# Attention stage of a macaron transformer layer: the softmax normalization is emitted one query tile later

## The chip, the cores and the metric

The kernel runs on all 8 cores of one Trainium2 chip. Each core takes one of the 8 sequences (2048 tokens x 1024 features) and computes the whole layer for it; the cores exchange nothing. The metric is device microseconds of the slowest core; lower is better.

## What is computed

```python
x = x + 0.5 * ffn(layernorm(x), W_fc, W_proj)
x = x + attn(layernorm(x), gamma, Wq, Wkv, Wo)
x = x + 0.5 * ffn(layernorm(x), W_fc, W_proj)

# ffn: h = relu(x @ W_fc.T)**2 ; y = h @ W_proj.T ; then a 5-step spiking
#      threshold on y (here five comparisons with constants)
# attn: 16 heads of 64, one shared key/value head, causal:
sim = einsum('bhid,bjd->bhij', q * SCALE, k)
sim = where(j > i, -max, sim)
out = einsum('bhij,bjd->bhid', softmax(sim), v)
return out.reshape(B, S, 1024) @ Wo
```

## The kernel before

The program is written as five instruction streams, one per engine: T (TensorE, PE), V (VectorE, DVE), A (ScalarE, ACT), S (SyncE, which issues DMAs) and G (GpSimd). `P.emit` appends an instruction to a stream and may raise a semaphore; `P.wait` makes a stream wait for a semaphore's value. Each engine executes its stream in the order in which it was emitted, so the order of the Python code is the order of the work.

Three stages follow each other: a feed-forward block, attention, and the second feed-forward block. The change is in the attention stage alone.

The attention loop goes over 16 query tiles (`qt`, 128 queries each). Tile `qt` needs keys 0 to `(qt+1)*128`, which are cut into `jbn` units of up to 512 keys: 1 unit for tiles 0 to 3, 2 for 4 to 7, 3 for 8 to 11, 4 for 12 to 15, 40 units in all. Only the last unit of a tile holds the diagonal; its width N is 128, 256, 384 or 512 columns.

For one unit:
- T computes the scores of 8 head pairs (lines 725, 730) into two alternating pairs of PSUM banks (0 to 3); a pair waits for the exponentials of the pair before the last, and for `v_mc` (line 723), which is raised inside the latest normalization.
- In the diagonal unit V adds a triangular mask (line 738) before A may read.
- A computes the exponential (line 753) into a buffer of WB and adds up the row sums in `sacc`. The first exponential of a tile waits for V's memset of its half of `sacc` (line 710, semaphore `v_sz`). `sacc` has two halves, by the parity of `qt`.
- S issues one DMA transpose for the whole unit (line 767) once all its exponentials are done and the previous unit's `emit_av` has freed the destination, which all units share.
- T multiplies the transposed exponentials with the values (`emit_av`, line 650), 4 matmuls per 128 keys, into banks 4 and 5 for even tiles and 6 and 7 for odd ones. This is emitted one unit late: after the scores of unit u comes `emit_av` of unit u-1.

When a tile's last unit has been through `emit_av`, `emit_msc(qt)` normalizes the tile: V reduces and inverts the row sums (lines 662, 666), T transposes them with 8 small matmuls (672), V copies (677, 680), T spreads them over the partitions with two matmuls (684), V copies again (689) and raises `v_mc` (692), and V multiplies the two output banks into HB (697, semaphore `v_msc`). It borrows the score banks that were used last, so T waits for all exponentials emitted so far (line 670). `emit_av` of a tile's first unit waits for `v_msc` of the tile before the last, whose banks it reuses.

After the loop come the output projection (line 798) and the second feed-forward block.

Of the kernel before, what the change touches and what calls it, by code (L numbers as in the profile page):

```python
# [61 lines left out]
def build_program(S=2048, stage="full"):  # L62
# [77 lines left out]
    def qs_t(pc, t0, n=512, p0=0, pn=128):  # L140
        return Q3[p0:p0 + pn, pc * S + t0: pc * S + t0 + n]
# [16 lines left out]
    def kt2_t(t0, n=512, p0=0, pn=128):  # L158
        return WB[p0:p0 + pn, KTP + t0: KTP + t0 + n]
# [4 lines left out]
    def p2_t(par, pc, hl, n=512):  # L164
        base = (P0P if par == 0 else P1P) + (pc * 2 + hl) * n
        return WB[:, base: base + n]
# [10 lines left out]
    def msc_t(c0, n):  # L177
        return WB[:, MSP + c0: MSP + c0 + n]

    def r2_t(c0, n):  # L180
        return WB[0:2, R2P + c0: R2P + c0 + n]
# [272 lines left out]
    def attention():  # L454
# [169 lines left out]
        unit_of = {}  # L624
        uidx = 0
        pend_av = None
        pend_msc = None

        def emit_av(qt, jb, u):
            ext = (qt + 1) * 128  # L630
# [26 lines left out]
        def emit_msc(qt):  # L657
            ob = 4 if qt % 2 == 0 else 6
            spb = 2 * (1 - (P.val("t_s") // 2) % 2)
            P.wait("V", "a_ex", ex_done[qt])  # L660
            po = (qt % 2) * 64
            P.emit("V", lambda E, po=po: E.tensor_reduce(
                rs16[:], sacc[:, po:po + 64].rearrange("p (g j) -> p g j", j=4),
                axis=mybir.AxisListType.X, op=ALU.add))
            P.drain("V")
            P.emit("V", lambda E: E.reciprocal(rs16[:], rs16[:]),
                   inc=("v_rs", 1))
            P.drain("V")
            P.wait("T", "v_rs", qt + 1)
            P.wait("T", "a_ex")  # L670
            for pc in range(NP):
                P.emit("T", lambda E, pc=pc, mb=spb: E.transpose(  # L672
                    PB[mb + pc // 4][0:2, (pc % 4) * 128:(pc % 4) * 128 + 128],
                    rs16[:, pc * 2: pc * 2 + 2], ident),
                    inc=("t_mst", 1) if pc == NP - 1 else None)
            P.wait("V", "t_mst", qt + 1)
            P.emit("V", lambda E, mb=spb: E.tensor_copy(  # L677
                r2_t(0, 512), PB[mb][0:2, 0:512]))
            P.drain("V")
            P.emit("V", lambda E, mb=spb: E.tensor_copy(  # L680
                r2_t(512, 512), PB[mb + 1][0:2, 0:512]), inc=("v_r2", 1))
            P.wait("T", "v_r2", qt + 1)
            for half in range(2):
                P.emit("T", lambda E, half=half, mb=spb: E.matmul(
                    PB[mb + half][:, 0:512], e2[:], r2_t(half * 512, 512),
                    start=True, stop=True), inc=("t_msm", 1) if half else None)
            P.wait("V", "t_msm", qt + 1)
            for half in range(2):
                P.emit("V", lambda E, half=half, mb=spb: E.tensor_copy(
                    msc_t(half * 512, 512), PB[mb + half][:, 0:512]))  # L690
                P.drain("V")
            P.emit("V", lambda E: E.engine_nop(), inc=("v_mc", 1))
            P.wait("V", "t_av", unit_of[(qt, ((qt + 1) * 128 + 511) // 512 - 1)] + 1)
            for half in range(2):
                dstbase = half * 4 * S + qt * 128
                dst3 = bass.AP(HB, dstbase, [[HB.shape[1], 128], [S, 4], [1, 128]])
                P.emit("V", lambda E, half=half, ob=ob, dst3=dst3: E.tensor_tensor(
                    dst3,
                    PB[ob + half][:, 0:512].rearrange("p (pc n) -> p pc n", n=128),
                    msc_t(half * 512, 512).rearrange("p (pc n) -> p pc n", n=128),  # L700
                    op=ALU.mult), inc=("v_msc", 1))
                P.drain("V")

        for qt in range(NQT):
            ext = (qt + 1) * 128
            jbn = (ext + 511) // 512
            par = qt % 2
            po = par * 64
            P.wait("V", "a_ex")
            P.emit("V", lambda E, po=po: E.memset(sacc[:, po:po + 64], 0.0),  # L710
                   inc=("v_sz", 1))
            for jb in range(jbn):
                u = uidx
                uidx += 1
                unit_of[(qt, jb)] = u
                upar = u % 2
                N = min(512, ext - jb * 512)
                for pc in range(NP):
                    i = P.val("t_s") // 2
                    bA = (i % 2) * 2  # L720
                    bB = bA + 1
                    P.wait("T", "a_ex", max(0, P.val("a_ex") - 2))
                    P.wait("T", "v_mc")
                    P.emit("T", lambda E, pc=pc, qt=qt, jb=jb, N=N, bA=bA:
                           E.matmul(PB[bA][:, 0:N],  # L725
                                    qs_t(pc, qt * 128, 128, 0, 64),
                                    kt2_t(jb * 512, N, 0, 64),
                                    start=True, stop=True))
                    P.emit("T", lambda E, pc=pc, qt=qt, jb=jb, N=N, bB=bB:
                           E.matmul(PB[bB][:, 0:N],  # L730
                                    qs_t(pc, qt * 128, 128, 64, 64),
                                    kt2_t(jb * 512, N, 64, 64),
                                    start=True, stop=True), inc=("t_s", 2))
                    diag = qt * 128 - jb * 512
                    if 0 <= diag < N:
                        P.wait("V", "t_s")
                        for b in (bA, bB):
                            P.emit("V", lambda E, b=b, diag=diag: E.tensor_add(  # L738
                                PB[b][:, diag:diag + 128],
                                PB[b][:, diag:diag + 128], tri[:]),  # L740
                                inc=("v_msk", 1))
                            P.drain("V")
                    if 0 <= diag < N:
                        P.wait("A", "v_msk")
                    P.wait("A", "t_s")
                    if jb == 0 and pc == 0:
                        P.wait("A", "v_sz")
                    if u >= 2 and pc == 0:
                        P.wait("A", "s_tr", tr_done[u - 2])
                    for hl in range(2):  # L750
                        g = pc * 2 + hl
                        P.emit("A", lambda E, hl=hl, par=upar, jb=jb, N=N,
                               b=(bA, bB)[hl], pc=pc, g=g, po=po: E.activation(  # L753
                                   p2_t(par, pc, hl, N), PB[b][:, 0:N],
                                   AF.Exp, bias=ncb[:, pc:pc + 1], scale=1.0,
                                   accum_out=sacc[:, po + g * 4 + jb:
                                                  po + g * 4 + jb + 1]),
                               inc=("a_ex", 1))
                P.wait("S", "a_ex")
                P.wait("S", "t_av", u)  # L760
                jcn = N // 128
                srcbase = P0P if upar == 0 else P1P
                src2 = bass.AP(WB, srcbase, [[WB.shape[1], 128], [1, 16 * N]])
                dst3 = bass.AP(WB, 0,
                               [[WB.shape[1], 128], [128, 16 * jcn], [1, 128]])
                P.emit("S", lambda E, dst3=dst3, src2=src2:
                       E.dma_start_transpose(dst3, src2), inc=("s_tr", 16))
                tr_done[u] = P.val("s_tr")
                if pend_av is not None:
                    pqt, pjb, pu = pend_av  # L770
                    emit_av(pqt, pjb, pu)
                    pext = (pqt + 1) * 128
                    if pjb == (pext + 511) // 512 - 1:
                        emit_msc(pqt)
                pend_av = (qt, jb, u)
            ex_done[qt] = P.val("a_ex")
        pqt, pjb, pu = pend_av
        emit_av(pqt, pjb, pu)
        emit_msc(pqt)
# [149 lines left out]
```

How the kernel before makes its waits and increments, by code:

```python
        def run(E, SEM, fn=fn, inc=inc):  # L45
            ins = fn(E)
            if inc is not None:
                ins.then_inc(SEM[inc[0]], inc[1])
# [2 lines left out]
    def wait(self, eng, name, val=None):  # L51
        v = self.val(name) if val is None else val
        if v <= 0:
            return
        self.streams[eng].append(
            lambda E, SEM, name=name, v=v: E.wait_ge(SEM[name], v))
```

## Time and profile before

| | us |
|---|---|
| median of 2 timed runs | 2202.68 (2197.27 to 2208.09) |
| profiled execution | 2202.2 |
| its span, slowest core (core 1) | 2200.7 |
| spans of the 8 cores | 2173.4 to 2200.7 |
| the attention loop on core 1 | about 907 to 1581 |

Busy shares of the span: PE 66%, PE weight loads 26%, DVE 36%, ACT 28%, POOL 4%. In the attention loop PE's granted clock reads 0.5 to 0.6 of full speed in most slices, while the feed-forward stages read 0.7 to 1.0. All numbers of the timeline are microseconds from the span's start on core 1. In a timeline row, the bracket holds the time for which the engine sat idle before the instruction, and what released it.

### The profile page before, as it was taken

Reading aid. Unit: us, or ns where it says so; the run is one execution under the profiler, and the core shown is the slowest. Engines: PE = TensorE matmul, PEld = TensorE weight load, DVE = VectorE, ACT = ScalarE, POOL = GpSimd, SP = SyncE. Lnnn points to the kernel's source line nnn. Section 1 sums busy time; section 2 is a strip of 40 time slices with the busy share of each in tenths; the row PEclk is TensorE's granted clock in tenths of the full one; section 3 lists DMA queues with packets and bytes.
Section 4 is the critical chain, followed back from the end, with each engine's and each line's share of the span. In section 5 each row is a group of like instructions: output and inputs, shape, how many; then the busy total and the mean of one; then the engine's idle time right before and its main releaser. Section 6 shows DMA issues by size and latency. Waiting matters only on the chain.

```text
span 2200.7 us, 20979 instructions; the slowest of 8 cores (2173.4 to 2200.7 us)
## 1 busy us (share of the span) xinstructions
PE 1448.8 (66%) x6244; PEld 574.2 (26%) x6244; DVE 790.6 (36%) x1530; ACT 616.2 (28%) x1644; POOL 78.2 (4%) x151
## 2 busy tenths in 40 slices
PE   0396769999963465344544554455494999999992
PEld 0032224444420111111111111111141444444441
DVE  0430056372536444443222111111145226363526
ACT  0320011111203000345565665667203303020200
POOL 2000100000020000000000000000100000000000
PEclk9788879999987879755555555565697999999996
DMA  9808912213050111054555666656722031313231
GB/s 234 159 1 210 194 36 64 99 39 115 36 123 3 22 22 21 10 86 86 111 106 109 118 121 124 115 110 130 157 75 89 7 134 49 134 65 121 78 110 58
DMA packets 315791, 202.54 MB, mean 92 GB/s; under 512 B 288394, under 2 KB 288522, under 8 KB 304418
## 3 DMA queue, kind: packets, MB, share of 16 engines
q1 hardware_dynamic: 293586, 104.28, 22.8%
q0 software_dynamic: 20944, 88.52, 15.1%
q10 hardware_dynamic: 1152, 8.39, 1.3%
q8 instruction: 55, 0.90, 0.2%
q14 instruction: 54, 0.44, 0.1%
HBM read 125.76 MB, written 25.25 MB: 69 GB/s over the span
## 4 chain that ended last, share of the span: by engine, by line
PE 49%; DMA 18%; DVE 16%; ACT 10%; issue 6%; DVEq 1%; POOL 0%; SPq 0%; ACTq 0%; POOLq 0%
PE pb L439 18%; PE pb L385 14%; ACT WB L753 8%; DMA WB<-WB 7%; PE pb L650 5%; DVE acc L332 4%; PE pb L533 3%; PE pb L798 3%; DMA Q<-wprojT 2%; DMA X<-xin 2%; DMA Q<-wp 2%; PE pb L725 1%; DMA R_t<-r_d 1%; ACT Q L391 1%; DVEq L59 1%
## 5 line engine op out<-in xcount | busy, mean ns | idle before, releaser
L385 PE MATMUL pb<-Q,WB 128*128 128x512 bf16 x2048 | 457.0, 384 | 84.0 <-DVE Q L360 55.8
L439 PE MATMUL pb<-HB,Q 128*128 128x512 bf16 x2048 | 452.7, 383 | 50.4 <-DMA Q<-wprojT 32.0
L753 ACT ACTIVATE WB<-pb,ncb 128x512 bf16<-128x512 f32 (+3 forms) x640 | 389.6, 643 | 243.4 <-PE pb L730 126.9
L391 ACT ACTIVATE Q<-pb 128x512 bf16<-128x512 f32 x256 | 152.9, 597 | 756.8 <-PE pb L385 672.0
L725 PE MATMUL pb<-WB,Q 64*128 64x512 bf16 (+3 forms) x320 | 153.1, 501 | 274.9 <-ACT WB L753 247.8
L385 PEld LDWEIGHTS pb<-Q,WB 128*128 128x128 bf16 x2048 | 199.3, 98 | 340.6 <-issue 112.5
L439 PEld LDWEIGHTS pb<-HB,Q 128*128 128x128 bf16 x2048 | 200.1, 99 | 303.0 <-issue 73.7
L394 DVE TENSOR_TENSOR HB<-Q 128x512 bf16<-128x512 bf16 x256 | 105.1, 424 | 191.6 <-ACT Q L391 184.5
L738 DVE TENSOR_TENSOR pb<-pb,tri 128x128 f32<-128x128 f32 x256 | 76.7, 300 | 251.5 <-PE pb L730 235.5
L730 PE MATMUL pb<-WB,Q 64*128 64x512 bf16 (+3 forms) x320 | 159.0, 520 | 0.0
L650 PE MATMUL pb<-WB 128*64 128x512 bf16 x544 | 122.5, 624 | 46.1 <-DMA WB<-WB 45.9
L753 ACT ACTIVATION_READ_ACCUMULATOR WB<-pb,ncb 128x1 f32 x640 | 143.4, 224 | 0.0
L332 DVE SCALAR_TENSOR_TENSOR acc<-pb,acc 128x512 f32<-128x512 f32 x192 | 132.9, 692 | 14.3
L725 PEld LDWEIGHTS pb<-WB,Q 64*128 64x128 bf16 x320 | 30.2, 101 | 407.3 <-issue 405.6
L227 PE MATMUL pb<-Q,ones 128*1 128x512 bf16 x96 | 40.3, 419 | 116.2 <-DVE Q L219 115.9
L224 ACT ACTIVATE Q<-X 128x512 bf16<-128x512 f32 x96 | 56.4, 623 | 208.8 <-PE pb L231 159.5
L445 DVE COPY ysb<-pb 128x512 f32<-128x512 f32 x8 | 5.5, 692 | 258.2 <-PE pb L439 258.1
L357 DVE TENSOR_TENSOR acc<-X,MU_t 128x512 f32<-128x512 f32 x64 | 44.3, 692 | 142.3 <-DMA R_t<-r_d 136.7
L677 DVE CAST WB<-pb 2x512 bf16<-2x512 f32 x16 | 10.9, 678 | 225.0 <-PE pb L672 225.0
L650 PEld LDWEIGHTS pb<-WB 128*64 128x64 bf16 x544 | 45.9, 165 | 105.8 <-issue 105.8
L219 DVE CAST Q<-X 128x512 bf16<-128x512 f32 x96 | 39.7, 423 | 74.0 <-DMA X<-xin 50.6
L798 PE MATMUL pb<-HB,WB 128*128 128x512 bf16 x256 | 57.5, 389 | 10.1 <-DMA WB<-wo 10.1
(89 smaller groups left out, 777.6 us busy)
## 6 DMA issues: line engine op xcount, KB each, us to landing
Q<-wp POOLq DMA_DIRECT2D x56, 1024.0 KB, 6.1
X<-xin SPq DMA_DIRECT2D x8, 1024.0 KB, 27.3
WB<-wfcT POOLq DMA_DIRECT2D x16, 512.0 KB, 50.8
Q<-wprojT POOLq DMA_DIRECT2D x32, 256.0 KB, 13.4
wp<-Q SPq DMA_DIRECT2D x8, 1024.0 KB, 9.0
wf<-WB ACTq DMA_DIRECT2D x8, 1024.0 KB, 15.9
WB<-wf POOLq DMA_DIRECT2D x8, 1024.0 KB, 20.2
xout<-X SPq DMA_DIRECT2D x32, 256.0 KB, 2.2
```

The lines of the kernel that those rows point to most:

```text
L332: P.emit("V", lambda E, dc=dc, i=i: E.scalar_tensor_tensor(acc[:], ysrc(), THETA[i], acc[:], ALU.is_ge, ALU.add))
L385: P.emit("T", lambda E, par=par, dc=dc, fc=fc: E.matmul(PB[par][:], wfc_t(dc, fc), xn_t(dc)[:], start=(dc == 0), stop=(dc == DC - 1)), inc ...
L391: P.emit("A", lambda E, par=par: E.activation(hh_t(par)[:], PB[par][:], AF.Relu), inc=("a_rl", 1))
L394: P.emit("V", lambda E, par=par, fc=fc: E.tensor_mul(h_t(fc), hh_t(par)[:], hh_t(par)[:]), inc=("v_h", 1))
L439: st=st, sp=sp: E.matmul(PB[dc][:], wpe_t(par, fcl, dc), h_t(fc), start=st, stop=sp), inc=mark)
L533: P.emit("T", lambda E, oc=oc, dc=dc, bank=bank: E.matmul(PB[bank][:], wq_t(dc, oc), a_t(dc)[:], start=(dc == 0), stop=(dc == DC - 1)), in ...
L650: st=st, sp=sp, ob=ob: E.matmul(PB[ob + half][hl * 64:(hl + 1) * 64, 0:512], vb_t(jc), rhs, start=st, stop=sp, skip_group_check=True, tile ...
L725: E.matmul(PB[bA][:, 0:N], qs_t(pc, qt * 128, 128, 0, 64), kt2_t(jb * 512, N, 0, 64), start=True, stop=True))
L730: E.matmul(PB[bB][:, 0:N], qs_t(pc, qt * 128, 128, 64, 64), kt2_t(jb * 512, N, 64, 64), start=True, stop=True), inc=("t_s", 2))
L738: P.emit("V", lambda E, b=b, diag=diag: E.tensor_add(PB[b][:, diag:diag + 128], PB[b][:, diag:diag + 128], tri[:]), inc=("v_msk", 1))
L753: b=(bA, bB)[hl], pc=pc, g=g, po=po: E.activation(p2_t(par, pc, hl, N), PB[b][:, 0:N], AF.Exp, bias=ncb[:, pc:pc + 1], scale=1.0, accum_ou ...
L798: P.emit("T", lambda E, pc=pc, dc=dc, tt=tt, bank=bank: E.matmul(PB[bank][:], wo_t(pc, dc), outT_t(pc, tt * 512, 512), start=(pc == 0), st ...
```

## The change

The pending normalization becomes a list. Where `emit_msc` was called right after a tile's last `emit_av`, the tile is now appended to the list. The list is emptied at the top of each tile, ahead of its memset, and once more after the loop, ahead of the last `emit_av`. Inside a tile, ahead of each `emit_av`, it is emptied down to one entry. `emit_msc` itself and everything else stay.

```diff
-        pend_msc = None
+        pend_msc = []
...
             po = par * 64
+            while pend_msc:
+                emit_msc(pend_msc.pop(0))
             P.wait("V", "a_ex")
             P.emit("V", lambda E, po=po: E.memset(sacc[:, po:po + 64], 0.0),
                    inc=("v_sz", 1))
...
                 tr_done[u] = P.val("s_tr")
+                while len(pend_msc) > 1:
+                    emit_msc(pend_msc.pop(0))
                 if pend_av is not None:
                     pqt, pjb, pu = pend_av
                     emit_av(pqt, pjb, pu)
                     pext = (pqt + 1) * 128
                     if pjb == (pext + 511) // 512 - 1:
-                        emit_msc(pqt)
+                        pend_msc.append(pqt)
                 pend_av = (qt, jb, u)
             ex_done[qt] = P.val("a_ex")
+        while pend_msc:
+            emit_msc(pend_msc.pop(0))
         pqt, pjb, pu = pend_av
         emit_av(pqt, pjb, pu)
         emit_msc(pqt)
```

## Rows read from the trace of the kernel before

**Rows 1.** The page: chain that ended last, by engine, whole span
```profile
PE 49%; DMA 18%; DVE 16%; ACT 10%; issue 6%; DVEq 1%; POOL 0%; SPq 0%; ACTq 0%; POOLq 0%
```
**Rows 2.** The chain cut to 905 to 1580 us, by line (answer ends so)
```profile
by line: ACT WB L753 26.1%; DMA WB<-WB 24.3%; PE pb L650 16.5%; issue 9.2%; PE pb L725 4.6%; PE pb L672 3.8%; DVE WB L689 3.1%; DVE pb L738 2.3%; DMA WB<-wo 2.0%; PE pb L684 1.8%; DVE WB L680 1.5%; DVE WB L677 1.5%; DVE HB L697 1.4%; DVEq L
```
**Rows 3.** Waits, 905 to 1580 us: who, for whom, total, times, longest
```profile
PE pb L650 <- DMA WB<-WB: 45.9, 15, 11.9
...
PE pb L684 <- DVE WB L680: 27.6, 16, 2.0
PE pb L725 <- DVEq L692: 27.1, 15, 1.8
```
**Rows 4.** Line 767, the 40 transposes of the loop
```profile
DMA to landing us min/median/max: 4.3/11.5/13.2
```
**Rows 5.** Timeline of PE, line 650: start, length, operation, idle before
```profile
1127.11 3.63 PE L650 MATMUL pb<-WB 128*64 128x512 bf16 x16 [2.13 <-DMA WB<-WB]
...
1162.59 3.63 PE L650 MATMUL pb<-WB 128*64 128x512 bf16 x16 [4.42 <-DMA WB<-WB]
...
1209.46 3.63 PE L650 MATMUL pb<-WB 128*64 128x512 bf16 x16 [2.78 <-DMA WB<-WB]
...
1254.84 3.63 PE L650 MATMUL pb<-WB 128*64 128x512 bf16 x16 [1.60 <-DMA WB<-WB]
...
1317.81 3.40 PE L650 MATMUL pb<-WB 128*64 128x512 bf16 x16 [2.43 <-DMA WB<-WB]
...
1507.12 2.78 PE L650 MATMUL pb<-WB 128*64 128x512 bf16 x12 [1.23 <-DMA WB<-WB]
...
1541.19 3.63 PE L650 MATMUL pb<-WB 128*64 128x512 bf16 x16 [2.40 <-DMA WB<-WB]
...
1571.96 3.63 PE L650 MATMUL pb<-WB 128*64 128x512 bf16 x16 [11.85 <-DMA WB<-WB]
```
**Rows 6.** Timeline of all engines: normalization of tile 6, then unit (7, 1)
```profile
1092.67 1.87 PE L672 MATMUL pb<-acc,rs 128*2 128x128 f32 x8
...
1096.23 1.00 PE L684 MATMUL pb<-WB,e 2*128 2x512 bf16 x2 [1.69 <-DVE WB L680]
...
1098.97 1.48 DVE L697 TENSOR_TENSOR HB<-pb,WB 128x512 bf16<-128x512 f32 x2 [0.17 <-issue]
...
1099.03 0.58 PE L725 MATMUL pb<-WB,Q 64*128 64x512 bf16 x1 [1.80 <-DVEq L692]
...
1100.61 0.69 DVE L738 TENSOR_TENSOR pb<-pb,tri 128x128 f32<-128x128 f32 x2 [0.16 <-issue]
```
**Rows 7.** Timeline of PE, line 672: tiles 7, 8 and 11
```profile
1130.67 1.87 PE L672 MATMUL pb<-acc,rs 128*2 128x128 f32 x8
...
1177.93 1.87 PE L672 MATMUL pb<-acc,rs 128*2 128x128 f32 x8 [0.96 <-ACT WB L753]
...
1321.14 1.03 PE L672 MATMUL pb<-acc,rs 128*2 128x128 f32 x8
```
**Rows 8.** Timeline: start of unit (4, 0), then of unit (8, 1)
```profile
983.35 0.58 PE L725 MATMUL pb<-WB,Q 64*128 64x512 bf16 x1 [1.80 <-DVEq L692]
...
984.97 0.11 DVE L710 MEMSET sacc<- 128x64 f32 x1 [0.21 <-issue]
...
985.23 0.69 ACT L753 ACTIVATE WB<-pb,ncb 128x512 bf16<-128x512 f32 x1 [8.02 <-DVE sacc L710]
...
1136.61 0.58 PE L725 MATMUL pb<-WB,Q 64*128 64x512 bf16 x1 [1.80 <-DVEq L692]
...
1137.37 0.69 ACT L753 ACTIVATE WB<-pb,ncb 128x512 bf16<-128x512 f32 x1 [10.58 <-PE pb L730]
```
**Rows 9.** Timeline: start of unit (9, 2), scores and first mask
```profile
1197.54 0.39 PE L725 MATMUL pb<-WB,Q 64*128 64x256 bf16 x1
...
1198.05 0.69 DVE L738 TENSOR_TENSOR pb<-pb,tri 128x128 f32<-128x128 f32 x2 [12.35 <-PE pb L730]
```
**Rows 10.** A stretch by windows: engines' busy us, clock, DMA share, GB/s
```profile
1199.00:1209.00 10.00, 2.16 (x12) 0.78 (x12) 4.30 (x16) 7.78 (x32) 0.00 (x0) 0.62 1.14 209
```

## The prediction

> **What bounds the kernel now.** I read the chain that ended last first, to find whether the stage that the change touches is on it. Over the whole span it is spread over three kinds of stage [rows 1]; cut to the attention loop (905 to 1580 us) it is ScalarE's exponentials (line 753), the DMA transposes (WB<-WB), and the attention-times-value matmuls (line 650), with the normalization's steps (lines 672, 677, 680, 684, 689, 697) behind them [rows 2]. No single engine bounds the loop: it is a relay. Then I read the waits of that stretch, to see where TensorE (PE) hands over [rows 3]: line 650 waits 45.9 us in 15 places for a transpose, and the normalization's hops cost a fixed wait each (27.6 and 27.1 us).
>
> Then the timeline, unit by unit. Write (q, j) for unit jb=j of query tile qt=q, S for its score matmuls, AV for its attention-times-value matmuls, TR for its transpose, msc for a normalization. After AV(u-1) ends, two things start together: S(u+1) with its exponentials, and TR(u). AV(u) needs both. S of a full unmasked unit takes 9.8 us; TR of a full unit lands 11.5 us after its issue (median) [rows 4], which makes 11.9 us from the end of one AV to the start of the next with the issue ahead and the release behind. So where nothing else stands between two AVs, PE waits for the transpose: full unmasked units with only S beside a full transpose waited six times, 2.13 us the first and 2.40 us the last, mean 2.4, once 3.0 [rows 5]. Where an msc stands between AV(u-1) and S(u+1), msc plus S exceed the transpose, and no wait is left.
>
> **What one msc costs on PE.** PE ran 8 small transposes (1.87 us), idled while VectorE (DVE) copied, ran 2 matmuls, idled again, and began S: 1092.67 to 1099.03, 6.4 us [rows 6]. Over the twelve msc(3) to msc(14) the gap between AV's end and the next S is 5.0 to 7.3 us, mean 6.2. The spread has two causes. After a short AV (4 matmuls), PE waits 0.96 us for the last exponentials [rows 7]. And the 8 transposes take 1.87 or 1.03 us, TensorE being at 1.2 or 2.4 GHz; after a 16-matmul AV both occur [rows 7], with total gaps 5.04, 5.87 and 5.10 us.
>
> **What the change does to the order.** msc(q) is queued after AV(q, last) as before, but emitted only at the top of tile q+2. For q = 0, 1, 2, tile q+1 has one unit, and the place is the same as before. The loop that empties the list while it holds more than one entry never fires, as the list is emptied at each tile's top. For q = 3 to 13, msc(q) moves from ahead of S(q+1, 1) to ahead of S(q+2, 0). It is still between an AV and an S in PE's in-order stream, and PE still waits in it for all exponentials. msc(14) comes just ahead of the last AV. Nothing is removed: same instructions, same bytes. What changes is which transpose runs beside the msc. For the numbers, Q is a tile and I compare its stretch from AV(Q-1, last-1) to AV(Q, 0).
>
> **A. The memset falls behind the multiplies: +12.3 us.** Tile q+2's first exponential waits for the memset of its sums (line 710), which DVE now reaches only after msc(q)'s two multiplies. The trace has this case: tile 4 follows msc(2), the memset runs at 984.97, and the first exponential starts 1.88 us after S begins, against 0.76 us where no memset is behind the multiplies [rows 8]. 1.12 us x 11 tiles (Q = 5 to 15) = 12.3. ScalarE paces S, so all of it is on the path.
>
> **B. Transposes lose their cover: +30.6 us.** S(Q, 1) now follows AV(Q-1, last) directly, with TR(Q, 0), always a full one, in flight. For Q = 8 to 15 that is the six-times-seen case, 2.4 us: 8 x 2.4 = 19.2. For Q = 4 to 7, unit (Q, 1) is the diagonal one with 128, 256, 384, 512 columns; the same pairs in later tiles waited 4.42, 2.78, 1.60 and about 0.1 us [rows 5], and with the spread of the transposes I take 4.0, 3.0, 1.5, 0.2: 8.7. Where the AV is the 4-matmul one (Q = 5, 9, 13) the exponentials, and so the transpose, are late by about 0.9 us more: 2.7.
>
> **C. The msc gaps: -13.8 us.** Before: 12 gaps on the path, 6.19 us each, 74.3. After: 11, since msc(14) now runs while TR(15, 3) is in flight, 11.85 us of idle PE [rows 5]. If that cover were gone it would cost its 6 us. The eleven now follow a 16-matmul AV, so no exponentials are waited for; the three such gaps give 5.0 to 5.9, and I take 5.5: 60.5.
>
> **D. Masks no longer queue behind the multiplies: -4.2 us.** In tiles 4 to 7, DVE's first mask add came 1.58 us after S began [rows 6], as it stood behind msc's multiplies; without an msc it comes 0.51 us after [rows 9]. 1.05 x 4.
>
> **E. Waits that the msc now covers: -5.8 us.** S(Q, 0) with TR(Q-1, last) in flight left AV waiting 2.13, 2.43 and 1.23 us (Q = 8, 12, 15) [rows 5]. With msc(Q-2) ahead of S these go.
>
> Sum: 12.3 + 30.6 - 13.8 - 4.2 - 5.8 = **+19.1 us**. Against the profiled execution (span 2200.7, its own time 2202.2, the rest outside the span) this gives 2221.3; that execution lies 0.5 below the median of the two timed runs, 2202.7, which gives 2221.8. I predict **2222 us**. Other stages hold none of the edited code and stay.
>
> **Bounds.** A: nothing if DVE were free earlier, but the row of tile 4 is the same instruction order, so 10 to 13. B: with every transpose at the median the waits are 0.25 us shorter each, -3; with every one at the slow end seen (12.3 landing, the 3.0 wait) +6. C: gaps all 5.1 give -4, all 6.4 (1.2 GHz throughout) +10. Together 2213 to 2239, and the two timed runs of before lie 11 us apart, which adds about 5 to each side.
>
> **Rivals.**
> *Nothing is late behind the msc (no change, 2203 us).* The swap is order for order: B would have to be offset by C and E. It decides if the msc gaps shrink to 4 us, for which no row speaks: two hops alone are 1.7 and 1.8 us [rows 3, 6]. Chance 0.07.
>
> *The uncovered transposes hide anyway (faster, 2191 us).* TR(Q, 0) would have to land within 9.8 us of its issue, so that S alone covers it. Then B is 0 and the sum is 12.3 - 13.8 - 4.2 - 5.8 = -11.5. For it: the queue is quiet before TR(Q, 0), the previous transpose having landed during the msc. Against it: the median of 11.5 us comes in quiet and busy stretches alike. Chance 0.04.
>
> The Trainium skill, Advanced Engine Details and Errata, section X-Bar Transpose (TRN2), says that transposing DMAs run as fast as plain ones, at 350 to 400 GB/s. An estimate from it: a full unit is 128 x 8192 x 2 bytes = 2.1 MB, some 5 to 6 us, and this rival would hold. A stretch inside one transpose shows 209 GB/s [rows 10], so the trace disagrees, and I keep the landing time measured.
>
> *The new stalls pull the clock and crowd the transposes (slower, 2241 us).* PE has eleven more idle gaps, so every msc may run at 1.2 GHz (+10), and one more transpose per tile starts right after another, each at the slow landing (+6), with 3 us from the extra idle in AV. It decides if msc's 8 transposes read 1.87 us in nearly all tiles. For it: ten of twelve read over 1.2 us now. Against it: two of the three that follow 16 matmuls read 1.03. Chance 0.11.
>
> *The order costs over 2% (above 2247 us).* That needs each moved msc to cost another 2.4 us, with no mechanism in sight. Chance 0.02.
>
> **How the numbers follow.** The forecast has 0.76. The range goes from 2210 to 2237, about its own bounds, and leaves most of the other three out (0.2). 2% is 44 us, about what a measurement of this kernel can tell from no change. Of all cases only the last exceeds it on the slow side; on the fast side the hidden transposes would have to come with more. I leave 0.01 on either side for what I have not seen: faster 0.01, within 2% 0.96, slower 0.03.
>
> **What would show it.** In the profile after: line 672's matmuls never wait for ScalarE; line 753 waits for the memset (L710) some 12 times rather than once; line 650's wait for WB<-WB rises from 45.9 us by about 30 less the 5.8 of E and the 6 that msc(14) takes out of the last wait, to 65 or 70 us, in some 24 places; DVEq's wait at line 725 stays near 1.8 us each. I am wrong if the wait for WB<-WB does not grow (B), if the first exponential of a tile starts under 1 us after its S (A), or if msc gaps fall under 5 us (C).

## The result and the profile after

| | us |
|---|---|
| before, median | 2198.15 (10 runs) |
| after, median | 2221.19 (11 runs) |
| ratio after / before | 1.0107, 95% interval 1.008 to 1.0134 |
| profiled execution after | 2215.5, span 2213.9 (core 0) |

The change made the kernel 1.1% slower, about 23.5 us (0.0107 x 2198). The medians, here and below, take in a few executions in which one die ran at a lower clock; the ratios leave them out.

To see whether the whole difference lies in the attention loop, I measured the loop on every core of a profile: from the first transpose's issue to the last small transpose of a normalization (line 672). Its mean over the 8 cores was 651.4 us before (649.3 to 653.4) and 674.4 us after (674.1 to 674.6): +23.0 us. The mean span of the 8 cores rose by 21.0 us, from 2185.5 to 2206.5, so the stages outside the loop added nothing. This "loop" is the yardstick for the experiments too, as it moves by a few us between cores where whole spans differ by 20.

In the changed kernel lines of the loop stand two lower down: scores are lines 727 and 732, exponentials 755, the memset 712. The first view is the chain that ended last, cut to 905 to 1600 us, by line (the answer ends so); it answers to [rows 2].

```profile
by line: DMA WB<-WB 39.2%; ACT WB L755 17.6%; PE pb L650 16.3%; issue 7.3%; PE pb L672 2.8%; DVE HB L697 2.8%; DVE WB L689 2.8%; PE pb L727 2.1%; DMA WB<-wo 2.0%; DVE pb L740 1.4%; DVE WB L680 1.4%; DVE WB L677 1.4%; PE pb L684 1.4%; DVEq L
```

The transposes went from 24.3% of the chain to 39.2%, and the exponentials from 26.1% to 17.6%. The multiplies of line 697 doubled their share, from 1.4% to 2.8%: they are on the path now. The waits of core 0 in that stretch (who, for whom, total us, times, longest) answer to [rows 3]:

```profile
ACT WB L755 <- DVE sacc L712: 133.1, 12, 13.9
...
PE pb L650 <- DMA WB<-WB: 68.9, 23, 8.0
...
PE pb L684 <- DVE WB L680: 27.3, 16, 2.0
PE pb L727 <- DVEq L692: 25.9, 14, 2.2
```

Two rows moved. The wait for a transpose rose from 45.9 us in 15 places to 68.9 us in 23 (mean of 8 cores 46.1 and 69.7). And ScalarE's wait at a tile's start now ends with the memset in 12 tiles, where before it did so once. The 133 us are not the memset's price; ScalarE idles through the whole normalization, and the memset only ends that wait last. The hops between PE and DVE inside the normalization are unchanged.

The timeline of core 0 shows one tile boundary, the normalization of tile 8 ahead of tile 10. It answers to [rows 8].

```profile
1206.32 1.87 PE L672 MATMUL pb<-acc,rs 128*2 128x128 f32 x8
...
1212.20 1.48 DVE L697 TENSOR_TENSOR HB<-pb,WB 128x512 bf16<-128x512 f32 x2 [0.17 <-issue]
...
1212.26 0.58 PE L727 MATMUL pb<-WB,Q 64*128 64x512 bf16 x1 [1.80 <-DVEq L692]
...
1213.88 0.11 DVE L712 MEMSET sacc<- 128x64 f32 x1 [0.21 <-issue]
...
1214.14 0.69 ACT L755 ACTIVATE WB<-pb,ncb 128x512 bf16<-128x512 f32 x1 [12.16 <-DVE sacc L712]
```

The scores begin at 1212.26, but the first exponential waits until 1214.14, 1.88 us, because the memset stands behind 1.48 us of multiplies. The next rows are the timeline of PE on core 0, line 650 and, at the loop's end, line 672; they answer to [rows 5]. The first is the value group of unit (9, 0), which had its transpose and only the next unit's scores ahead of it:

```profile
1187.34 3.63 PE L650 MATMUL pb<-WB 128*64 128x512 bf16 x16 [2.99 <-DMA WB<-WB]
...
1568.95 3.63 PE L650 MATMUL pb<-WB 128*64 128x512 bf16 x16 [2.05 <-DMA WB<-WB]
1572.51 1.63 PE L672 MATMUL pb<-acc,rs 128*2 128x128 f32 x8
...
1584.37 3.41 PE L650 MATMUL pb<-WB 128*64 128x512 bf16 x16 [7.95 <-DMA WB<-WB]
```

The first row is a place where the kernel before did not wait at all. The last rows show the one normalization that became free: tile 14's sits between two value groups 11.8 us apart (1572.58 to 1584.37), which is the 11.85 us of the last transpose in [rows 5], no longer.

### The profile page after: what moved, and what is told of

The parts are those of the page before. It is cut to its first block, busy times and chain, and to the rows that moved or that the text cites. A ratio compares the mean times of both kernels' runs of the same rounds, so it can differ in the third digit from the quotient of the medians.

```text
span 2213.9 us, 20884 instructions; the slowest of 8 cores (2200.3 to 2213.9 us)
## 1 busy us (share of the span) xinstructions
PE 1439.7 (65%) x6149; PEld 575.9 (26%) x6244; DVE 791.2 (36%) x1530; ACT 616.8 (28%) x1644; POOL 78.2 (4%) x151
## 4 chain that ended last, share of the span: by engine, by line
PE 48%; DMA 21%; DVE 16%; ACT 7%; issue 5%; DVEq 1%; SPq 0%; POOL 0%; ACTq 0%; another core or an unknown queue 0%; POOLq 0%
PE pb L439 18%; PE pb L385 14%; DMA WB<-WB 12%; ACT WB L755 6%; PE pb L650 5%; DVE acc L332 4%; PE pb L804 3%; PE pb L533 3%; DMA X<-xin 2%; DMA Q<-wprojT 2%; ACT Q L391 1%; DVEq L59 1%; DMA R_t<-r_d 1%; DVE X L335 1%; PE pb L227 1%
## 5 line engine op out<-in xcount | busy, mean ns | idle before, releaser
L439 PE MATMUL pb<-HB,Q 128*128 128x512 bf16 x2008 | 448.4, 383 | 47.2 <-DMA Q<-wprojT 30.6
L727 PE MATMUL pb<-WB,Q 64*128 64x512 bf16 (+3 forms) x320 | 155.7, 509 | 280.1 <-ACT WB L755 254.1
L650 PE MATMUL pb<-WB 128*64 128x512 bf16 x544 | 123.0, 626 | 69.0 <-DMA WB<-WB 68.9
L732 PE MATMUL pb<-WB,Q 64*128 64x512 bf16 (+3 forms) x320 | 161.6, 527 | 0.0
L332 DVE SCALAR_TENSOR_TENSOR acc<-pb,acc 128x512 f32<-128x512 f32 x192 | 132.9, 692 | 14.3
L804 PE MATMUL pb<-HB,WB 128*128 128x512 bf16 x250 | 57.6, 392 | 11.8 <-DMA WB<-wo 11.5
L533 PE MATMUL pb<-HB,WB 128*128 128x512 bf16 x250 | 60.7, 384 | 0.6 <-issue 0.5
## 6 DMA issues: line engine op xcount, KB each, us to landing
X<-xin SPq DMA_DIRECT2D x8, 1024.0 KB, 27.4
```

The lines of the kernel that those rows point to most:

```text
L332: P.emit("V", lambda E, dc=dc, i=i: E.scalar_tensor_tensor(acc[:], ysrc(), THETA[i], acc[:], ALU.is_ge, ALU.add))
L439: st=st, sp=sp: E.matmul(PB[dc][:], wpe_t(par, fcl, dc), h_t(fc), start=st, stop=sp), inc=mark)
L533: P.emit("T", lambda E, oc=oc, dc=dc, bank=bank: E.matmul(PB[bank][:], wq_t(dc, oc), a_t(dc)[:], start=(dc == 0), stop=(dc == DC - 1)), in ...
L650: st=st, sp=sp, ob=ob: E.matmul(PB[ob + half][hl * 64:(hl + 1) * 64, 0:512], vb_t(jc), rhs, start=st, stop=sp, skip_group_check=True, tile ...
L727: E.matmul(PB[bA][:, 0:N], qs_t(pc, qt * 128, 128, 0, 64), kt2_t(jb * 512, N, 0, 64), start=True, stop=True))
L732: E.matmul(PB[bB][:, 0:N], qs_t(pc, qt * 128, 128, 64, 64), kt2_t(jb * 512, N, 64, 64), start=True, stop=True), inc=("t_s", 2))
```

## The experiments

Eight runs, four on one chip and four on another, each beside runs of the kernel before. "After" below is the changed kernel. Each loop is read from one profile, and the profiles come from different chips; b_split, profiled on both, read 619.9 and 619.6 us.

### a_memset: the memset taken out from behind the multiplies

```diff
# in emit_msc, right behind the reciprocal:
+            if clear:
+                P.wait("V", "a_ex")
+                P.emit("V", lambda E, po=po: E.memset(sacc[:, po:po + 64], 0.0),
+                       inc=("v_sz", 1))
# at the tile's top:
-            while pend_msc:
-                emit_msc(pend_msc.pop(0))
-            P.wait("V", "a_ex")
-            ... memset
+            if pend_msc:
+                emit_msc(pend_msc.pop(0), clear=True)
+            else: ... wait and memset as before
```

> Changed kernel, with one edit: at a tile's top the memset of the row sums is issued inside the normalization, right behind the reciprocal, so it is no longer behind the two multiplies. The loop (first transpose issue to last small transpose of line 672, mean of 8 cores) is 674.4 us in the changed kernel and 651.4 us before. Theory (the memset's place costs 1.1 us in 11 tiles, and ScalarE paces the unit): loop 662, time 12 us under the changed kernel, and no wait of line 753's exponentials for the memset. Rival (the exponentials are not what the unit waits for, the transposes are): loop stays within 3 us of 674.

Measured: 2209.01 us median, ratio to before 1.0052 (1.0016 to 1.0087); loop 659.3 us, 15.1 under after. The timeline of its core 7, again ahead of tile 10:

```profile
1205.17 0.11 DVE L671 MEMSET sacc<- 128x64 f32 x1 [0.61 <-ACT WB L760]
...
1215.21 1.48 DVE L701 TENSOR_TENSOR HB<-pb,WB 128x512 bf16<-128x512 f32 x2 [0.17 <-issue]
1215.28 0.58 PE L732 MATMUL pb<-WB,Q 64*128 64x512 bf16 x1 [1.80 <-DVEq L696]
...
1216.10 0.69 ACT L760 ACTIVATE WB<-pb,ncb 128x512 bf16<-128x512 f32 x1 [11.08 <-DMA WB<-WB]
```

The memset is done 10 us early, and the exponential starts 0.82 us after the scores instead of 1.88. The rival falls: ScalarE does pace this unit. The gain is more than the 12 us expected. Tile by tile on core 0 of both runs, whose loops differ by 14.3 us, the scores of the first unit take 9.8 to 9.9 us in tiles 4 to 15, where after took 10.9 (11.3 once). That is 11.9 us in the eleven tiles of the prediction and 1.1 us in tile 4, which had the memset behind multiplies in the kernel before too [rows 8]. The rest has little to do with the memset: tiles 2 and 3 gave 0.13 us each, and the normalizations of tiles 1 and 2 were 1.7 us shorter together, as their 8 small transposes took 1.46 and 1.28 us instead of 1.86 and 1.87.

### a_half: the uncovered transposes made short

```diff
-                src2 = bass.AP(WB, srcbase, [[WB.shape[1], 128], [1, 16 * N]])
+                nh = 8 if jb == 0 and jbn > 1 else 16
+                src2 = bass.AP(WB, srcbase, [[WB.shape[1], 128], [1, nh * N]])
# and nh * jcn for 16 * jcn in dst3
```

> Changed kernel, leaving work out: the transpose of each tile's first unit (tiles 4 to 15) moves only half of its columns, so the output is not the reference's. Theory (the uncovered transposes cost 32 us): a half transpose lands after some 6.7 us and hides behind the scores; loop 674 - 32 = 642 us, the wait of line 650 for WB<-WB falls from 69 to some 37 us or less. Rival (attention-times-value waits for something else that the trace books on the transpose): loop stays near 674.

This kernel leaves out half of those transposes' columns, so it serves to measure a cost and is no repair. Measured: 2184.52 us median, ratio to before 0.9959 (0.9939 to 0.9979); loop 640.6 us, 33.8 under after. The wait row of its slowest core:

```profile
PE pb L650 <- DMA WB<-WB: 39.0, 12, 8.6
```

From about 70 us in 23 places to 39 in 12: eleven waits went (of the twelve tiles, tile 7's was 0.17 us), and with them the whole time that was expected. The transpose was what these matmuls waited for.

### a_cover: as late, but in another place

```diff
# tile's top: only reduce and reciprocal of the pending tile (part 1), then the memset
-            while pend_msc:
-                emit_msc(pend_msc.pop(0))
+            if pend_msc:
+                emit_msc(pend_msc[0], part=1)
# behind the value matmuls of the tile before, ahead of the second unit's scores
+                        if pend_msc:
+                            emit_msc(pend_msc.pop(0), part=2)
                         pend_msc.append(pqt)
```

> Changed kernel, but only the row sums' reduce and reciprocal stay at the tile's top; the rest of the deferred normalization is issued one unit later, ahead of the scores of the tile's second unit, where the first unit's full transpose is in flight. It stays one tile late, as in the changed kernel. Theory (the loss is the place, not the lateness): the transposes are covered again and the memset is early, and one normalization less lies on the path than before: loop 651.4 - 6 to 8 = 644 us, 30 us under the changed kernel. Rival (normalizing a tile late is itself what costs): loop near 670.

Measured: 2195.02 us median, ratio to before 0.9988 (0.9964 to 1.0013), so no change against before that can be told; loop 647.0 us, 27.4 under after and 4.4 under before. Its wait row is that of the kernel before almost to the digit (46.4 us, 15 places):

```profile
PE pb L650 <- DMA WB<-WB: 46.4, 15, 8.1
```

The normalization is still one tile late, and the loss is gone. Being late costs nothing; the place does. The 4.4 us are less than the 6 to 8 expected. The equal wait rows hide two moves that cancel: the wait ahead of the last value group fell from 11.85 us to 8.1, and the others rose, on core 1 from 34.1 us to 38.3. Three of them carry that rise, 1.3 to 1.5 us each, and there the transpose landed 12.79, 13.16 and 13.04 us after its issue, where it took 11.55, 11.86 and 11.53 in the kernel before. The last section comes back to such late landings.

### b_split and b_split2: the kernel before with its transposes in halves

```diff
-                P.wait("S", "a_ex")
-                P.wait("S", "t_av", u)
...
+                for half in range(2):
+                    P.wait("S", "a_ex", ex_half if half == 0 else None)
+                    P.wait("S", "t_av", 2 * (u - 1) + half + 1)
+                    src2 = bass.AP(WB, srcbase + half * 8 * N, ...)
+                    dst3 = bass.AP(WB, half * 4096, ...)
+                    P.emit("S", ... dma_start_transpose(dst3, src2),
+                           inc=(f"s_tr{half}", 16))
# emit_av: all matmuls of half 0 behind s_tr0, then those of half 1 behind s_tr1;
# t_av is raised after each half
```

> Kernel before, with each unit's transpose issued as two halves on two semaphores (head pairs 0 to 3, then 4 to 7) and the attention-times-value matmuls in the same order, each half waiting for its own transpose only; the second unit's half can start when the first half's matmuls are done. Theory (transposes are a late partner of the scores by 2.4 us, no throughput bound): the waits of 34 us inside the loop go and the last one shrinks by some 4: loop 613 to 620 us. Rival (a transpose has a fixed cost, 4.3 us landing for the narrowest, that two halves pay twice): loop 640 us or more.

> The kernel of b_split again, for its time beside the other three: loop 620 us, time 2152 to 2165 us.

Measured: loop 619.9 and 619.6 us in the two profiles, 31.5 and 31.8 under before. The time of b_split2 was 2164.42 us (median of 5 runs), ratio 0.986 (0.9806 to 0.9914). Of b_split's four runs the profiled one took 2151.96 us; the others took 2228.42 to 2256.38 us, and no ratio could be formed. In b_split the transposes' line (80 of them) and line 650's wait for them read:

```profile
  PE pb L650: 9.9, 4
DMA to landing us min/median/max: 3.0/6.7/8.4
```

The waits fell from 46 to 10 us. Two halves with a fixed cost each still hide. The first half of the next unit is issued in the middle of a value group (core 2: at 1263.10, 2.0 us after the group's start at 1261.09) and not behind its end 3.6 us after its start, and the second half is not needed before the first half's matmuls are done. The rival falls. In the chain cut to 905 to 1600 us the transposes have 3.2%, and SyncE's instructions that issue them 2.1%. The edit also regroups the value matmuls, all of one half before the other, where the expectation speaks of the same order; a group of 16 still takes 3.63 us where nothing is waited for, so the regrouping cost nothing.

### a_split: the changed kernel with its transposes in halves

The edit is that of b_split, made on after.

> Changed kernel with the transposes in two halves, as in the run b_split, where the loop fell from 651.4 to 619.9 us. Here deferral is compared without the transposes on the path. Theory (transposes that lose their cover carry the loss): against b_split the deferral now costs only the memset's 12 us and gives back the shorter gaps (some 14) and the masks (4): loop 612 to 620 us, 55 us or more under the changed kernel's 674.4. Rival (deferral costs of itself, whatever the transposes): loop 23 us over b_split, 643.

Measured: 2160.86 us median, ratio to before 0.9832 (0.9792 to 0.9873); loop 617.7 us, 56.7 under after and 2 under the 619.6 to 619.9 of b_split. Its waits for the memset and for transposes:

```profile
ACT WB L757 <- DVE sacc L713: 107.8, 12, 11.2
...
PE pb L650 <- DMA WB<-WB: 7.5, 8, 3.1
```

This run separates the two causes from the order itself. The same deferral that cost 23.0 us with whole transposes gains 2 us with halves, though the memset is still behind the multiplies. So the loss needs the transposes to be late. The 2 us are a reading of the loop alone; the ratios of the whole time, 0.9832 here and 0.986 for b_split2, have intervals that overlap.

### b_both: the normalization opened

```diff
# emit_msc ends after the two copies (v_r2); the rest is emit_msc_b,
# called behind the next unit's first score pair and its exponentials:
+                    if pc == 0 and pend_msc is not None:
+                        emit_msc_b(*pend_msc)
+                        pend_msc = None
```

> Kernel before, transposes in two halves, and the normalization opened around the next unit's first score pair: the 8 small transposes, then the first pair's scores (they use the other two banks), then the two spreading matmuls; only the second pair waits for v_mc. Theory (the hops between TensorE and VectorE idle ScalarE for the whole gap, and one pair's exponentials, 1.33 us, fit into it 15 times): loop 619.9 - 20 = 600 us. Rival (the next wait takes its place, VectorE's masks and copies or the transposes): loop within 5 us of b_split's 619.9.

Measured: loop 600.9 us, 19.0 under b_split; time 2167.77 us median, 2144.33 the fastest, ratio 0.9816 (0.9757 to 0.9875). The loop did what was expected. The whole time did not follow in this run: beside b_split2's 0.986 the intervals overlap, and the slowest core's span is 2166.3 where the others have 2123.3 to 2156.6, which the loop, 600.0 to 602.9 on all cores, does not explain. They lie ahead of the loop: from the span's start to the first transpose's issue, cores 4 and 5 took 935.3 and 940.5 us at a granted clock of 0.853, the other six 903.9 to 917.5 us at 0.875 to 0.885.

### a_best: the changed kernel repaired

Transposes in halves, memset early, normalization opened.

> Changed kernel with three repairs: transposes in two halves, the memset right behind the reciprocal, and the normalization opened around the first score pair. Theory: with no transpose and no memset on the path, the late place keeps its own gains over b_both (masks no longer behind the multiplies 4 us, no wait for the exponentials behind short value matmuls, the last but one normalization beside the last transpose, shorter gaps): loop some 10 us under b_both, about 590 us, time about 2130. Rival (the late place has no gain of its own): loop equal to b_both's.

Measured: 2127.97 us median, ratio to before 0.9662 (0.9632 to 0.9692), faster than both kernels; loop 585.7 us, 15.2 under b_both and 65.7 under before. The timeline of its core 5 shows the opened normalization:

```profile
1174.41 1.22 PE L676 MATMUL pb<-acc,rs 128*2 128x128 f32 x8
1175.57 0.39 PE L740 MATMUL pb<-WB,Q 64*128 64x512 bf16 x1
...
1176.22 0.69 ACT L769 ACTIVATE WB<-pb,ncb 128x512 bf16<-128x512 f32 x1 [3.31 <-PE pb L745]
...
1177.32 0.59 PE L693 MATMUL pb<-WB,e 2*128 2x512 bf16 x2 [1.36 <-DVE WB L684]
...
```

The first pair's scores and exponentials (1175.57, 1176.22) now stand between the small transposes and the spreading matmuls, where PE and ScalarE idled before. In this kernel the late place is worth 15 us over the early one, more than the 10 expected. Most of that is what the prediction listed under C: on core 1 of both runs, whose loops differ by 14.7 us, the gaps from a value group's end to the scores' second pair come to 61.1 us in 11 places against 74.2 in 12 for tiles 3 to 14. How the rest divides was not traced.

## Why the prediction was right

Forecast 2222 us, within 2%, slightly slower; measured 2221.19. The mechanism was right, but that the number is off by 1 us only is luck: two errors cancelled. The move is 23.5 us where 19.1 were summed, and the kernel before, on which the sum was put, has a median of 2198.15 us over ten runs where its first two gave 2202.68. The stated range, 2210 to 2237, is also narrower than the prediction's own bounds, 2213 to 2239 with about 5 us more on either side. Point by point, on core 0 of the profile after:

- **Order.** As told: the same instructions, and tiles 4 to 15 the ones that changed. Line 672 waits for ScalarE in none of the eleven moved normalizations. "Never" was too much, as it still does in tiles 0 and 1 (1.12 and 0.48 us), whose place is the old one.
- **A, +12.3.** In the eleven tiles the scores of the first unit take 10.9 us from first to last (11.3 once) against the 9.8 of a unit without a memset behind multiplies. a_memset took back 11.9 of it in these tiles.
- **B, +30.6.** Line 650's waits beside the second unit's scores were 4.56, 3.44, 3.18 and 0.17 us in tiles 4 to 7 and 2.18 to 3.06 in tiles 8 to 15: together 31.7. The three behind the 4-matmul groups (tiles 5, 9, 13) are 2.99 to 3.44. a_half took away 33.8. The sum fits better than its terms: tile 6 was put at 1.5 us and waited 3.18, its transpose having landed after 13.18 us, and tiles 5, 9 and 13 waited less than the 3.3 to 3.9 summed.
- **C, -13.8.** The eleven gaps were 5.0 to 5.9 us, 59.7 in sum against 60.5. Tile 14's normalization was free.
- **D, -4.2.** The diagonal units of tiles 4 to 7 took 8.0, 9.4, 10.5 and 11.8 us, each 0.8 to 1.3 less than before: 4.0.
- **E, -5.8.** In tiles 8, 12 and 15 the value group behind the first unit's scores no longer waits.

Put together, the measured terms give 31.7 + 12.3 - 14.6 - 4.0 - 5.8 = 19.6. The 3.4 us that are left to 23.0 have two visible parts. Waits that the sum held fixed moved: the one ahead of the last transpose from 0.23 us to 2.05, one in tile 13 from 2.42 to 3.69, others slightly down, +1.1 net; the transposes behind these two landed after 13.29 and 13.03 us where they had taken 11.53 and 11.58. And the sum was made on core 1, whose loop before was 1.2 us above the mean of the eight, while after all cores agree within 0.5. About 1 us stays unassigned.

The rivals: no change needed gaps of 4 us and falls with C's 5.0 to 5.9; a hidden transpose falls with B's waits; more than 2% falls with the ratio. Lower clock falls too: the 8 small transposes took 1.87 us in 2 of the 11 moved normalizations, not in nearly all.

By the Trainium skill, Advanced Engine Details and Errata, section X-Bar Transpose (TRN2), the uncovered transposes should have landed in 5 to 6 us (an estimate from its 350 to 400 GB/s). In the profile after, the twelve uncovered ones landed 11.46 to 13.18 us after their issue, median 11.5, so 2.1 MB / 11.5 us = 182 GB/s; the measurement decides.

## What to carry to other kernels

Before moving a piece of work along an in-order stream, ask what transfer was in flight beside it: the piece may be the only thing that hides it, and the new place may hide one that was never late. Look also at what small instruction (here a memset of 0.11 us) ends up behind the moved work on the other engines. If the transfer is the late partner, cut it in two along the order in which it is consumed; after that the deferral turned from a loss of 23 us into a gain, of 2 us as it stood and of 15 with the memset early and the normalization opened.

## What the hardware showed that I had not expected

SyncE (SP) is occupied for most of a transpose's time. The rows are the transposes' line in the kernel before (40 of them) and in b_split (80): duration on SP in ns (min/median/max).

```profile
L767 SPq DMA_TRANSPOSE WB<-WB x40: 1847/9772/10403, 924.3 to 1560.2; - x40
```

```profile
L773 SPq DMA_TRANSPOSE WB<-WB x80: 1231/4802/5327, 906.9 to 1514.6; - x80
```

SP was occupied for 9.8 of the 11.5 us from issue to landing, and for 4.8 of 6.7 with half the columns. So about 1.8 us of either lies behind the issue, and two halves back to back occupy SP for 9.6 us, no longer than one whole. That fits inside a unit's scores and value matmuls, 13.4 us (9.8 + 3.6), so cutting a transpose in two cost nothing here. The bytes move in the same time: of the transpose issued at 1197.70 on core 1 of the kernel before, which held SP until 1207.40 and landed at 1209.22, the DMA engines moved 13 GB/s in the microsecond from 1198, 215 from 1199, 218 from 1207 and 129 from 1208. Whether the issue or the copying sets the pace, these rows cannot tell; no run tested it.

Some whole transposes took longer: in the kernel before six of the 40 on core 1 landed after 12.1 to 13.2 us, at scattered places. The DMA queues tell them apart. Beside the transposes' own queue, two queues that the profile names "instruction" (q8 and q14) moved a packet now and then, of 16 or 8 KB. I sorted the full transposes of all 8 cores by whether such a packet started between issue and landing (us from issue to landing):

| | full transposes | with no such packet | with one or more |
|---|---|---|---|
| before | 224 | 133: 11.46 to 11.58 | 91: 11.46 to 13.19, 55 of them over 11.6 |
| after | 224 | 85: 11.46 to 11.56 | 139: 11.45 to 13.33, 92 of them over 11.6 |

Not one late transpose is without such a packet, though 36 and 47 with one were on time. The changed kernel met more of them, which agrees with the waits that moved in the sum above. That the packets delay the transposes is what this suggests; no run tested it.
